# Middle stage of a three-stage kernel: residual through TensorE's identity, joined and reordered products on VectorE, joined products on GpSimd

## The reference

```python
xw = xw + pos                                  # windows as sequences of 64 steps
x, z = split(seq @ W_in)                       # 64 channels to 2 x 128
x = silu(conv1d(x) + conv_b)
dt, Bm, Cm = split(x @ W_xproj)                # 4, 16, 16
dt = softplus(dt @ W_dt + b_dt)
# for each of 128 channels and 16 states, along the 64 steps:
h = exp(dt * A) * h + (dt * u) * B             # the scan
y = sum over states of h * C, + u * Dp
out = (y * silu(z)) @ W_out
x = x + out                                    # the residual
```

## Time and profile before

| | |
|---|---|
| median of 3 runs | 8556.24 us (8542.18 to 8576.54) |
| the profiled execution's own time | 8588.41 us |
| its span in the profile | 8586.6 us |
| middle stage, first to last scan | 2614.1 to 8069.1 us |
| busy: TensorE matmuls / VectorE / ScalarE / GpSimd | 6282.9 / 6791.2 / 4293.2 / 5185.6 us |

### The profile page before, as it was taken

One profiled execution on the slowest core, in us unless ns is written; L12 is line 12 of the kernel. 1 busy time (PEld: TensorE's weight loads), 2 busy tenths in 40 slices (PEclk: granted clock), 3 DMA queues, 4 the chain that ended last, 5 costly groups with the idle time before them and its releaser, 6 DMA issues. The chain is left out here.

```text
span 8586.6 us, 102988 instructions
## 1 busy us (share of the span) xinstructions
PE 6282.9 (73%) x30668; PEld 2512.8 (29%) x30668; DVE 6791.2 (79%) x7924; ACT 4293.2 (50%) x5876; POOL 5185.6 (60%) x1723
## 2 busy tenths in 40 slices
PE   6888888888876777676776767777777777777455
PEld 3444444444431222222222222222222222222133
DVE  3555555555547999999999999999999999999634
ACT  1222222222225666666666666666666666666400
POOL 0000000000007999999999999999999999999500
PEclk8889889898977888888888888888888888888666
DMA  1111111111114655656556566565655656565553
GB/s 33 41 42 41 45 39 43 42 40 45 41 36 172 206 196 194 209 184 205 197 195 208 184 202 198 194 211 185 209 192 195 207 190 211 187 202 197 143 154 125
DMA packets 513971, 1253.45 MB, mean 146 GB/s; under 512 B 170085, under 2 KB 172297, under 8 KB 513673
## 3 DMA queue, kind: packets, MB, share of 16 engines
q1 hardware_dynamic: 513417, 1252.41, 45.2%
q0 software_dynamic: 512, 0.53, 0.0%
HBM read 943.30 MB, written 231.21 MB: 137 GB/s over the span
## 5 line engine op out<-in xcount | busy, mean ns | idle before, releaser
L1185 DVE TENSOR_TENSOR_SCAN b_h<-b_a,b_h 128x448 f32<-128x448 f32 x3584 | 3673.9, 1074 | 101.6 <-ACT b_a L1114 95.3
L1023 POOL TENSOR_TENSOR b_h<-b_h,b_ct 128x1792 f32<-128x1792 f32 x896 | 3571.1, 3989 | 279.6 <-DVE b_h L1185 265.8
L1114 ACT ACTIVATE b_a<-b_dts,decay 128x441 f32<-128x441 f32 x3584 | 2225.4, 629 | 1587.2 <-DVE b_h L1185 1560.3
L1035 POOL MEMSET b_seq<- 128x938 f32 x2 | 1.7, 880 | 2496.6 <-POOLq L798 2496.6
L1175 DVE TENSOR_TENSOR b_h<-b_dus,b_b 128x896 f32<-128x896 f32 x1344 | 1434.7, 1068 | 62.0 <-DMA b_dus<-d_dtu 60.6
L1282 PE MATMUL b_b<-b_rows,spread_b 16*128 16x512 f32 (+1 forms) x1792 | 567.6, 652 | 886.4 <-DVE b_h L1175 885.3
L1009 POOL TENSOR_TENSOR b_h<-b_dus,b_bt 128x896 f32<-128x896 f32 x448 | 933.9, 2085 | 44.8 <-DMA b_bt<-d_rows 28.1
L1290 PE MATMUL b_y<-b_h,fold 128*32 128x512 f32 (+1 forms) x7168 | 951.4, 658 | 8.1 <-POOL b_h L1023 8.1
L495 DVE TENSOR_TENSOR a_xg<-a_xd,a_pb 128x784 f32<-128x784 f32 x512 | 495.3, 967 | 519.4 <-PE a_pb L609 517.3
L1251 PE MATMUL b_w<-b_seq,w_conv 128*128 128x384 f32 (+1 forms) x896 | 557.4, 786 | 12.6 <-DMA b_seq<-b_seq 12.6
L1243 PE MATMUL b_w<-b_u,wx 128*64 128x512 f32 x448 | 361.1, 961 | 212.5 <-DVE b_dt L1207 212.5
(11 more groups left out here) (211 smaller groups left out, 8586.9 us busy)
## 6 DMA issues: line engine op xcount, KB each, us to landing
b_bt<-d_rows SPq DMA_DIRECT2D x448, 448.0 KB, 6.0
b_ct<-d_rows SPq DMA_DIRECT2D x448, 448.0 KB, 3.9
b_dts<-d_dt SPq DMA_DIRECT2D x448, 448.0 KB, 5.7
b_dus<-d_dtu SPq DMA_DIRECT2D x448, 448.0 KB, 6.2
a_xd<-a_xn SPq DMA_DIRECT2D x256, 196.0 KB, 3.4
d_dt<-b_dt SPq DMA_DIRECT2D x112, 448.0 KB, 2.5
d_dtu<-b_soft SPq DMA_DIRECT2D x112, 448.0 KB, 2.6
b_seq<-b_seq SPq DMA_DIRECT2D x112, 234.0 KB, 6.4
```

The lines of the kernel that those rows point to most:

```text
L1023: nc.gpsimd.tensor_tensor(two, two, ct[t // 4 % 2][:].unsqueeze(1).broadcast_to([P, 2, TB]), ALU.mult).then_inc(hc_done, 2)
L1114: a(steps(bank(aa, k)), steps(half(dts[t % 4], k)), ACT.Exp, scale=decay[:, t % 4, t // 4:t // 4 + 1]).then_inc(a_done, 1)
L1185: v.tensor_tensor_scan(half(hh[t], k), bank(aa, k), half(hh[t], k), 0.0, ALU.mult, ALU.add).then_inc(h_done, 1)
```

## The change

It has five parts, all in `phase_b`. First, the residual: TensorE adds `xr` into `b_w` by a matmul with the identity ahead of the output products, and ScalarE copies the sum into `x3s` behind its exponentials of tile 13, in place of VectorE's addition. Second, `dus` and `bt` become single tiles, and VectorE makes the products b of tiles 1 and 2, and of 6 and 7, in one instruction each. Third, VectorE's order: a product now stands behind scans by the table `after`, the gate product stands behind product 6,7 and the step behind scan 8. Fourth, ScalarE's order: the norm's end, the silu block, the softplus functions and the moves of `xp` and `z` change their tile. Fifth, GpSimd makes the products b of rows 0 and 1 in one instruction, and those of rows 2 and 3; its step product stands one tile later, and SyncE issues the loads of `bt` and of `dus[0]` for the next unit ahead of `load_ct(3)`. Ahead of the loop the gate's product comes last.

```diff
-                dus = ring("dus", 4)
-                bt = ring("bt", 2)
+                dus = sb("dus", [P, 4, TB])
+                bt = sb("bt", [P, 2, TB])
...
+                                sp.wait_ge(pb_done, row_no(i, 3, it))
+                                sp.wait_ge(rows_stored[par], stored)
+                                load_bt(0, par)
+                                load_bt(1, par)
+                                sp.wait_ge(dtu_stored[par], stored)
+                                load_dus(0, par)
...
-                            pool.wait_ge(bt_in[m % 2], it * 64 + (32 * i + 16 * (m // 2)))
-                            pool.wait_ge(folded, row_no(i, m, it) - 4)
-                            nc.gpsimd.tensor_tensor(hh[4 * m], dus[0][:], bt[m % 2][:], ALU.mult).then_inc(pb_done, 1)
+                            for b in range(2):
+                                pool.wait_ge(bt_in[b], it * 64 + (32 * i + 16 * (m // 2)))
+                            pool.wait_ge(folded, row_no(i, m + 1, it) - 4)
+                            nc.gpsimd.tensor_tensor(h_all[:, 4 * m:4 * m + 5:4, :], dus[:, 0:1, :].broadcast_to([P, 2, TB]), bt[:],
+                                                    ALU.mult).then_inc(pb_done, 2)
...
-                                if t in (3, 7):
-                                    inputs(i, 2 + t // 4, it)
-                                if t in (13, 15) and more:
-                                    inputs(1 - i, t // 15, it + i)
+                                if t == 4:
+                                    inputs(i, 2, it)
+                                if t == 13 and more:
+                                    inputs(1 - i, 0, it + i)
...
-                                if t == 7 and more:
+                                if t == 8 and more:
                                     step_input(1 - i, spot(i, "pre", it, kind))
...
+                        def residual(c, q):
+
+                            act.wait_ge(made, c + 2)
+                            act.wait_ge(x3_stored, 16 * q)
+                            a(win(x3s), seqs(ww), ACT.Copy).then_inc(moved, 1)
...
-                                if t == 2 and norms:
+                                if t == 1 and norms:
                                     norm_end(spot(0, "var", it, kind))
                                 if t == 0 and finals:
                                     final_start(spot(1, "xc2", it, kind), it - 1)
-                                if t == 2 and finals:
+                                if t == 1 and finals:
                                     final_end(spot(1, "var2", it, kind))
-                                if t == 4:
+                                if t == 5:
                                     silus(i, it, kind, o)
-                                if t == 5 and more:
+                                if t == 6 and more:
                                     act.wait_ge(dtu_stored[i], 16 * it + 16 * i)
                                     softplus_start(spot(i, "pre", it, kind))
-                                if t == 6 and more:
+                                if t == 7 and more:
                                     softplus_end(o + 1)
-                                if t == 9 and more:
+                                if t == 10 and more:
 
                                     act.wait_ge(bt_spread, row_no(i, 0, it) - 1)
                                     act.wait_ge(rows_stored[1 - i], 16 * it)
                                     move(spot(i, "xp", it, kind), rows[1 - i][:], rows=4 * NS)
-                                if t == 11 and more:
+                                if t == 12 and more:
                                     act.wait_ge(yz_ready, o - 1)
                                     move(spot(i, "z", it, kind), gate[1 - i][:])
+                                if t == 13 and i == 0 and kind != FIRST:
+                                    residual(spot(0, "out", it, kind), it - 1)
...
-                        def inputs(t, i, it):
-
-                            if t < 4:
-                                dve.wait_ge(dus_in[t], 16 * unit_no(i, it))
-                            if t % 4 == 1:
-                                dve.wait_ge(bt_spread, row_no(i, t // 4, it))
-                                dve.wait_ge(folded, row_no(i, t // 4, it) - 4)
-                            v.tensor_tensor(hh[t], dus[t % 4][:], bb[:, 0:TB], ALU.mult).then_inc(b_done, 1)
+                        def inputs(lo, hi, i, it):
+
+                            for t in range(lo, hi):
+                                if t < 4:
+                                    dve.wait_ge(dus_in[t], 16 * unit_no(i, it))
+                            if lo % 4 == 1:
+                                dve.wait_ge(bt_spread, row_no(i, lo // 4, it))
+                                dve.wait_ge(folded, row_no(i, lo // 4, it) - 4)
+                            v.tensor_tensor(h_all[:, lo:hi, :], dus[:, lo % 4:lo % 4 + hi - lo, :],
+                                            bb[:, 0:TB].unsqueeze(1).broadcast_to([P, hi - lo, TB]), ALU.mult).then_inc(b_done, hi - lo)
...
-                            dve.wait_ge(x3_stored, 16 * q)
-                            dve.wait_ge(xr_loaded, 16 * q)
-                            v.tensor_tensor(win(x3s), seqs(ww), win(xr), ALU.add).then_inc(moved, 1)
...
+                            after = {0: (1, 3), 1: (3, 4), 4: (5, 6), 5: (6, 8), 7: (9, 10), 9: (10, 11), 10: (11, 12),
+                                     12: (13, 14), 13: (14, 15), 14: (15, 16)}
                             for t in range(UNIT):
-                                if t % 4:
-                                    inputs(t, i, it)
-                                if not (kind == FIRST and i == 0 and t == 0):
-                                    scan_before(t, i, it)
+                                scan(t, i, it)
+                                if t in after:
+                                    inputs(*after[t], i, it)
                                 if t == 5 and not (kind == FIRST and i == 0):
                                     gated(1 - i, row_no(i, 0, it) - 1, unit_no(i, it) - 1)
-                                if t == 14 and i == 0 and kind != FIRST:
-                                    residual(spot(0, "out", it, kind), it - 1)
-                                if t == 7 and not (kind == LAST and i == 1):
+                                if t == 8 and not (kind == LAST and i == 1):
...
-                        def out_proj(c, o):
+                        def out_proj(c, o, q):
 
                             pe.wait_ge(yz_ready, o)
+                            pe.wait_ge(xr_loaded, 16 * q)
                             pe.wait_ge(moved, c + 1)
+                            by_seq = xr[:].rearrange("p (r w c) -> p w r c", r=WS, c=WS)
                             for lo, hi in banks(TB):
+                                mm(ww[:, lo:hi], ident[:], by_seq[:, lo // ST:hi // ST], start=True, stop=False)
                                 for i in range(2):
-                                    last = mm(ww[C * i:C * i + C, lo:hi], w_out_t[:], yz[i][:, lo:hi], start=True, stop=True)
+                                    last = mm(ww[C * i:C * i + C, lo:hi], w_out_t[:], yz[i][:, lo:hi], start=False, stop=True)
```

41 lines of the change are left out of this document (13 added, 28 removed).

## The result

The changed kernel takes 8681.17 us (median of 4 runs, 8677.35 to 8695.81); the kernel before, run beside it, 8566.39 (4 runs, 8542.18 to 8587.2). The ratio is 1.0138, 95% interval 1.0107 to 1.017: slower by 115 us, where 8405 was forecast, and outside the range.

The account below looks back on a forecast made before the run. VectorE and GpSimd were both taken as nearly full. GpSimd's 36.35 plus VectorE's 45.2 and 10.8 gave 92.35, with counted waits 94.7 us a turn against 97.41, scaled to 8405 us; range 8300 to 8550.

Parts of the forecast that it names:

- Every product b at 0.98 from start to start: On VectorE, each single product b was priced at 0.98 us from one instruction's start to the next.
- R: Even unit, scan 14: wait for exponentials behind ScalarE's residual copy, between nothing and 3.1 us, taken as 1.2, mostly hidden.
- The GpSimd-bound leg of 36.35: Even unit: GpSimd works without a gap from scan 3's end to the next unit's joined product, 36.3 us; scan 0 waits.
- odd start: Scans 1 and 2 of the odd unit: waits of 2.4 us if TensorE is slow, taken as 1.1 a turn.
- even start: Scans 1 and 2 of the even unit: 0.2 us wait at TensorE's full clock, 0.9 and 0.9 at the lower; 0.7 taken.
- softplus end: Behind exponentials 7 on ScalarE: a new wait of 0.4 us in each unit, the even unit's hidden.
- the gate product's wait: VectorE's wait for TensorE's fold before the gate product, 2.24 us a turn, would go once moved behind product 6,7.
- the silu block: ScalarE's silu functions, 4.75 us against 4.87 of VectorE work beside them: covered, no wait.
- a join on VectorE: Two products b in one VectorE instruction: 1.92 us, saving 0.05 an element, 0.2 in a turn.
- GpSimd's join: Products b joined on GpSimd cost 3.96 us, saving 0.5 a turn; bounds 0 and 0.5.
- The residual off VectorE, -0.98: Taking the residual addition off VectorE saves it 0.98 us in a turn.
- the slower one: Rival, chance 0.11: TensorE at its lower clock wherever ScalarE waits for it; turn 98.6 us, +65 us, 8620.

## Why the prediction was wrong, by its own steps

- *Every product b at 0.98 from start to start.* This is the first step that failed. The earlier trace rows has a product whose next scan is that of another tile, and I used its price for 14 products a turn that stand directly ahead of their own scan. They cost 1.18 to 1.19: 2.2 to 2.8 us in a turn, none forecast. The run with six pairs a turn in the kernel before shows the price, 66 us where 67 was expected. That the changed kernel would be faster by this much without its pairs is not shown: both runs that set pairs apart in it were slower, by other waits.
- *R, the exponentials of tile 14 behind the copy: 1.2, hidden by GpSimd, 0.1 counted.* The second step that failed, and in its mechanism: the size was near (1.80), but it was not hidden. The sum gives GpSimd 36.35 us from the end of scan 3 to its joined product for the odd unit, and VectorE 34.4 for the same stretch and so 1.95 us of room. Measured over 48 turns, GpSimd needs 37.2 and VectorE 37.9, so that VectorE comes last and scan 0 of the odd unit does not wait. Five direct pairs (1.0), R and the wait at scan 8 (0.3) are more than the room. Moving the copy gave 84 us, 1.5 a turn. Among its signs of being wrong the prediction names this place, with over 2 us.
- *The GpSimd-bound leg of 36.35.* It exists, but behind the rest: with the copy late, scan 0 waits 1.0 us a turn for GpSimd, within the 1 to 2 forecast. GpSimd is busy 92% of the window, not over 96%.
- *The other waits*: odd start 1.26 against 1.1; even start 1.48 against 0.7; softplus end 0.53 against 0.8, of which 0.4 counted; and a load ahead of product 1,2, 0.56 against none. Together 3.8 against 2.2 counted. The even start is the half clock of the centring strip: the prediction priced it at 1.8 and the full clock at 0.2 and took 0.7 between them; measured are 1.88 and 0, and four turns in five are slow. In the odd unit I expected a shorter pause of TensorE to keep its strip fast in over half of the turns; it was slow in all, at 1.26 where the sum for slow ones had 2.4.
- *Right*: the gate product's wait went; the silu block is covered (5012.26 to 5015.18 without a gap); a join on VectorE is worth 0.04 to 0.05, 1.92 from start to start (5012.26 to 5014.18). GpSimd's join, forecast at up to 0.5 a turn, gave 0.9976 by itself, about 0.4 a turn, which the interval does not tell from nothing. The Trainium skill ("VectorE: DVE Perf Modes", the section on the TRN2 errata) gives an instruction of VectorE with a PSUM source 120 cycles and one for each element at 0.96 GHz; an estimate from this is 1.06 us for a single product and 1.99 for a joined one. The trace agrees with it as a duration (1.06 and 2.00), while from start to start the rows have 0.98 and 1.92.
- *The residual off VectorE, -0.98.* It pays 0.8 a turn inside the changed kernel, costs 0.8 in the kernel before with the copy at 13, and pays 0.4 there with the copy at 15. In the kernel before, the copy's place decides the sign.

The sum again, with VectorE's work as the prediction counted it: 91.6 - 0.98 - 0.2 = 90.4; direct pairs up to 2.8; waits for ScalarE 5.1, for the load 0.6: 98.9 of the 99.49 measured, and up to 0.6 less by what the two share. The forecast of 94.7 had 90.4, 1.95 from GpSimd's leg, 2.3 of waits.

Among the rivals the slower one came nearest in time (8620, 61 us too low), and part of its mechanism is there. TensorE's mean clock was no lower, but at the strips that ScalarE waits for it was at or near half: ahead of the even unit in 38 of 48 turns (50 of 50 before), ahead of the odd one in 48 of 48 (45 of 49 before). What the rival does not have is the direct pairs. How much of the copy's own wait for TensorE is clock and how much is order, no run here parts. Likewise open is why the products' order costs more alone than together with ScalarE's, beyond the waits that were counted.

## What to carry to other kernels

Price an instruction from a row in which its neighbours are those that it will have: a consumer directly behind its producer on one engine is another case than one with an instruction in between. When an operation moves to an engine that issues in order, list what stands behind it there, and try it one or two places later before judging it. If a stretch is said to be hidden behind another engine, compare the room with the sum of all that may fall into it. In a kernel with two engines at 95%, change one part at a time: here neither order was cheap alone, and the best version was the old order with the residual's move (its copy late), GpSimd's joins and two joins of VectorE in other rows.

## What was not expected of the hardware

On VectorE a 128x896 f32 product directly ahead of the scan that reads it takes 1.18 us from start to start, with another tile's scan behind it 0.98, at the same duration of 1.06; in the trace the product ends at 5026.56 and its scan starts at 5026.69, a gap without a releaser, where others overlap by 0.08. A joined product pays the same 0.2: directly ahead of its scan it takes 2.12 to 2.14 us in the run with four pairs set apart, ahead of another instruction 1.91.

```profile
5033.60 2.02 DVE L1185 TENSOR_TENSOR b_h<-b_dus,b_b 128x1792 f32<-128x1792 f32 x1 [3.35 <-issue]
5035.74 1.09 DVE L1196 TENSOR_TENSOR_SCAN b_h<-b_a,b_h 128x448 f32<-128x448 f32 x1
```

In the changed kernel, TensorE's clock at the same strip, behind the same pause of 1.81 us, was 0.50 in one turn and 1.00 in another, and a wait of 2.9 us hangs on it.
